# Graph product with layer norm: the product chunks of a pair of units gathered beside one lower row

## The chip, the cores and the metric

The kernel runs on one core of one Trainium2 chip. The metric is the device time of one execution in microseconds (us). The profile adds what each engine did: PE is TensorE's matrix work, PEld its weight loads, DVE is VectorE, ACT ScalarE, POOL GpSimd, SP SyncE, which issues most of the loads.

## The reference

For each of 8 batches there are x (2048x64) and adj (2048x2048). U (2048x16) gives one gate matrix for all batches.

```
Ws = 0.5 * (W + jnp.swapaxes(W, -1, -2))
A = jax.nn.sigmoid(U @ U.T)
K = Ws * A[None, :, :]
deg = jnp.maximum(K.sum(axis=-1), EPS)
d = jax.lax.rsqrt(deg)
K = K * d[:, :, None] * d[:, None, :]
return w_scale * jnp.einsum('bnm,bmc->bnc', K, x)
```

The result is added to x, and each row of 64 is normalised (mean, variance). All is in float32.

## The kernel before

**Tiles.** A batch's adj is cut into 4x4 units of 512x512, each held in a tile K[(i, j)] as four rows (r = 0 to 3) of 128x512. A unit has one home; the next batch's unit is loaded over it when its product is done.

**Lower rows.** The work of a batch goes over 40 lower rows (`LOWER`, 10 steps of 4 rows). For lower row g, TensorE transposes the mirrored blocks into a bank of the tile tw (L280: 4 transposes of 128x128, on a diagonal step 1, 2, 3 and 4, that is on rows 0 to 3, 8 to 11, 32 to 35 and 36 to 39). VectorE adds tw to K's row ("add g", L481), and then multiplies by the gate with a row sum ("gate g", L491). VectorE's order is add g, gate g-1, add g+1, gate g. tw has three banks, so that transposes of row g wait for add g-3 (`bank_free`, L270).

**Upper rows.** Row r of step s is, at row number 4(s+1)+r+2 (six after its lower row), transposed back into the tile kt (L294, 4 transposes; on diagonal steps 3, 2, 1, 0) and copied by ScalarE with a row sum (L410). The first of a step waits for all four gates of its step (L289): the upper row at row 14 for gate 11, at 18 for gate 15, at 26 for gate 23, at 34 for gate 31.

**Products.** The einsum is 16 unit products, in 8 pairs (`PAIRS`), each pair in four chunks c. One chunk is one call of `product`: two matmuls with 64 columns of output each, one on either half of the array (L309, 128x512 moving), two records each. Pairs 0 to 3 of batch b run beside its own lower rows (`OWN_ROWS`; `FIRST_OWN_ROWS` in batch 0), pairs 4 to 7 are carried into batch b+1 (`CARRIED_ROWS`). The three lists give for each of 16 chunks the number of the lower row. Rows 40 to 45 have no lower row: upper rows and products alone.

**Order.** TensorE's order at one row number is: tw transposes, product chunks listed for it, kt transposes. At row 5 stand eight transposes of y of batch b-2 before those of tw (L332), whose results VectorE scales (L528). GpSimd adds x, centres and divides (L222, L226, L233) beside VectorE's rows; mean and variance are taken by VectorE at rows 11 and 15. Degrees and z (L499, L511) stand at rows 24 and 25, 33 and 34, and at the end of a batch.

**Loads.** SP loads a pair's units of the next batch when `prod_done` says that the pair is finished (L192). VectorE, ScalarE, GpSimd and SP have written orders too. Batches 0 and 1 are written out apart (no y of an earlier batch in batch 1, no carried products in batch 0); batches 2 to 7 are the loop. Batch 7's carried pairs stand behind the loop (L390).

Of the kernel before, what the change touches and what calls it, by code (L numbers as in the profile page):

```python
# [14 lines left out]
G = 4  # L15
# [41 lines left out]


OWN = 4
OWN_ROWS = [28, 28, 30, 31, 32, 33, 34, 36, 38, 39, 39, 40, 45, 45, 45, 45]  # L60
FIRST_OWN_ROWS = [28, 29, 30, 31, 32, 33, 34, 35, 36, 38, 39, 40, 45, 45, 45, 45]
CARRIED_ROWS = [2, 4, 4, 5, 7, 8, 10, 11, 13, 15, 17, 18, 18, 21, 22, 24]
UPPER_LAG = 2


# [21 lines left out]
def bass_graph_resnorm_kernel(nc, x, adj, u, w_scale, out):  # L87
# [6 lines left out]
    with ExitStack() as ctx:  # L94
# [167 lines left out]
        def _(pe):  # L262
# [35 lines left out]
            def product(b, q, c, stage=2):  # L298

                if c == 0:  # L300
                    if q in Z_OF_PAIR:
                        pe.wait_ge(z_ready, NZ * b + (Z_OF_PAIR[q] + 1))
                    if q == 0 and stage == 0:
                        pe.wait_ge(gate_ready, NL)
                    elif q == 0:
                        pe.wait_ge(y_copied, 2 * b)
                for n, m in PAIRS[q]:
                    at = (m % 2) * C
                    t = pe.matmul(yp[at:at + C, m // 2, :], z[:, n * G + c, :], K[(n, m)][:, c, :],  # L309
                                  start=(q == first_unit[m] and c == 0), stop=(q == last_unit[m] and c == G - 1))  # L310
                if c == G - 1:
                    t.then_inc(prod_done, 1)
# [22 lines left out]
            def outer_product(g):  # L335

                s, r = LOWER[g]
                i, j = STEPS[s]
                if g >= 2:
                    pe.wait_ge(gate_ready, g - 1)  # L340
                w = lower_width(s, r)
                pe.matmul(yp[:, g % 2, 0:w], ut_a[:, (i * G + r) * P:(i * G + r + 1) * P],  # L342
                          ut_b[:, j * UW:j * UW + w], start=True, stop=True).then_inc(uu_done, 1)

            def steps(b, stage):
# [3 lines left out]
                for at in range(NL + G + 2):  # L349
# [4 lines left out]
                    if at < NL and stage == 0:  # L354
                        for g in range(gates_before(at), gates_before(at + 1)):
                            outer_product(g)
                    for part, row in zip(carried, CARRIED_ROWS):
                        if row == at and stage:
                            product(*part, stage=stage)
                    for part, row in zip(own, OWN_ROWS if stage else FIRST_OWN_ROWS):  # L360
                        if row == at:
# [292 lines left out]
```

## Time and profile before

| what | value |
| --- | --- |
| time, median of 3 runs | 559.32 us (559.29 to 559.76) |
| span of the profiled execution | 557.6 us |
| PE busy | 95% of the span, 3208 instructions |
| VectorE busy | 78%, 1113 instructions |
| ScalarE busy | 39% |
| GpSimd busy | 18% |
| DMA | 142.98 MB, mean 256 GB/s |

The span runs from the first to the last instruction of the profiled execution; the median time of the runs is 1.7 us longer, which is what lies around the span. A time of the trace is counted from the span's start. Busy times of TensorE contain overlaps of pipelined matmuls.

### The profile page before, as it was taken

What the parts mean: (1) busy time and instruction counts of PE and PEld (TensorE: products, weight loads), DVE (VectorE), ACT (ScalarE), POOL (GpSimd) and SP (SyncE); (2) the same over time, 40 slices, a digit from 0 to 9 for tenths busy, and PEclk for the clock granted to TensorE, in tenths of its full rate; (3) what the DMA queues carried; (4) which work ended last, traced back from release to release, by engine and by line L of the source; (5) the groups of instructions that cost most, each with busy time, mean ns of one, the idle gap of its engine ahead of it and who ended that gap; (6) DMA issues with size and microseconds to landing.
All of it is one profiled execution on the core that took longest, in us unless ns stands there. A gap on an engine that the chain in (4) does not pass through costs nothing.

```text
span 557.6 us, 9999 instructions
## 1 busy us (share of the span) xinstructions
PE 530.7 (95%) x3208; PEld 296.0 (53%) x3208; DVE 433.7 (78%) x1113; ACT 217.9 (39%) x654; POOL 99.3 (18%) x61
## 2 busy tenths in 40 slices
PE   4899999999999999999999999999999999999991
PEld 4685445654556545555456544665456554564430
DVE  5898566875999659985799759997599956997554
ACT  2894413532245414344145332444134531444311
POOL 0000010001150013300214011410133002130153
PEclk9999999999999999999999999999999999999997
DMA  8997899758977699578985879776996688945003
GB/s 272 387 332 274 292 341 300 248 207 297 338 250 244 215 352 316 211 201 291 356 280 209 269 275 352 226 260 201 356 319 240 188 299 320 321 171 168 1 0 75
DMA packets 102850, 142.98 MB, mean 256 GB/s; under 512 B 37296, under 2 KB 37296, under 8 KB 102832
## 3 DMA queue, kind: packets, MB, share of 16 engines
q1 hardware_dynamic: 88240, 139.08, 71.7%
q10 hardware_dynamic: 14592, 3.67, 3.6%
q8 instruction: 10, 0.16, 0.1%
q14 instruction: 8, 0.07, 0.0%
HBM read 138.54 MB, written 4.19 MB: 256 GB/s over the span
## 4 chain that ended last, share of the span: by engine, by line
PE 80%; DVE 8%; issue 6%; ACT 3%; POOL 1%; DMA 1%; POOLq 0%; DVEq 0%
PE yp L309 39%; PE kt L294 21%; PE tw L280 17%; DVE k L481 3%; DVE k L491 2%; ACT k L410 1%; ACT gate L401 1%; PE yp L342 1%; DMA h<-in_L_gnn_U_dram 1%; PE tw L332 1%; DVE h L528 1%; DVE z L511 1%; PE tw L374 0%; POOL h L222 0%; PE yp L374 0%
## 5 line engine op out<-in xcount | busy, mean ns | idle before, releaser
L410 ACT ACTIVATE k<-kt 128x512 f32<-128x512 f32 (+3 forms) x288 | 151.7, 528 | 297.5 <-PE kt L294 292.6
L309 PE MATMUL yp<-k,z 128*64 128x512 f32 x960 | 247.5, 612 | 2.8 <-DVE z L511 2.8
L481 DVE TENSOR_TENSOR k<-tw,k 128x512 f32<-128x512 f32 (+2 forms) x320 | 193.4, 606 | 33.8 <-PE tw L280 30.5
L491 DVE CUSTOM_DVE_ANT_0 k<-k,gate 128x512 f32<-128x512 f32 (+2 forms) x320 | 217.2, 681 | 0.3 <-ACT gate L401 0.3
L294 PEld LDWEIGHTS kt<-ident,k 128*128 128x128 f32 x960 | 106.2, 140 | 128.7 <-ACT k L410 90.3
L280 PE MATMUL tw<-ident,k 128*128 128x128 f32 x1088 | 169.5, 275 | 2.7 <-DVE k L481 1.2
L294 PE MATMUL kt<-ident,k 128*128 128x128 f32 x960 | 157.8, 282 | 1.7 <-ACT k L410 1.7
L280 PEld LDWEIGHTS tw<-ident,k 128*128 128x128 f32 x1088 | 126.1, 140 | 30.5 <-issue 13.2
L309 PEld LDWEIGHTS yp<-k,z 128*64 128x64 f32 x960 | 52.1, 135 | 64.2 <-issue 58.6
L239 POOL TENSOR_TENSOR d<-deg,minus_half 128x4 f32<-128x4 f32 (+1 forms) x24 | 29.2, 1217 | 316.8 <-DVE deg L501 316.8
L410 ACT ACTIVATION_READ_ACCUMULATOR k<-kt 128x1 f32 x288 | 57.1, 198 | 0.0
L499 DVE TENSOR_REDUCE deg<-deg_parts 128x4 f32<-128x20 f32 (+1 forms) x24 | 4.3, 181 | 47.8 <-ACT k L410 47.8
L231 POOL TENSOR_TENSOR rstd<-var,minus_half 128x16 f32<-128x16 f32 x7 | 20.4, 2911 | 36.3 <-DVE var L542 36.3
L491 DVE DVE_READ_ACCUMULATOR2_ANT deg_parts<- 128x1 f32 x320 | 25.9, 81 | 0.0
L511 DVE TENSOR_TENSOR z<-xt,d 128x256 f32<-128x256 f32 (+1 forms) x24 | 12.4, 515 | 16.7 <-POOL d L239 16.7
L222 POOL TENSOR_TENSOR h<-h,x_keep 128x1024 f32<-128x1024 f32 x7 | 16.5, 2357 | 47.3 <-DVE h L528 47.3
L226 POOL TENSOR_TENSOR h<-h,mean 128x1024 f32<-128x1024 f32 x7 | 13.3, 1901 | 47.4 <-DVE mean L535 47.4
L401 ACT ACTIVATE gate<-yp 128x512 f32<-128x512 f32 (+3 forms) x40 | 20.4, 552 | 1.7 <-PE yp L342 1.2
L342 PE MATMUL yp<-ut_b,ut_a 128*128 128x512 f32 (+3 forms) x40 | 16.1, 439 | 1.3 <-ACT gate L401 1.1
L233 POOL TENSOR_TENSOR h<-h,rstd 128x1024 f32<-128x1024 f32 x7 | 15.9, 2269 | 0.5
L390 PE MATMUL yp<-k,z 128*64 128x512 f32 x64 | 14.2, 595 | 0.0
L528 DVE TENSOR_TENSOR h<-tw,f 128x512 f32<-128x512 f32 x14 | 9.0, 686 | 3.7 <-PE tw L332 3.7
(60 smaller groups left out, 116.3 us busy)
## 6 DMA issues: line engine op xcount, KB each, us to landing
k<-in_adj_dram SPq DMA_DIRECT2D x128, 1024.0 KB, 7.2
xt<-in_x_dram ACTq DMA_DIRECT2D x7, 512.0 KB, 7.0
out_dram<-h SPq DMA_DIRECT2D x7, 512.0 KB, 8.7
xt<-in_x_dram SPq DMA_DIRECT2D x1, 512.0 KB, 14.1
out_dram<-k SPq DMA_DIRECT2D x2, 256.0 KB, 2.6
h<-in_L_gnn_U_dram SPq DMA_DIRECT2D x1, 128.0 KB, 4.3
ws<-in_L_gnn_w_scale_dram ACTq DMA_DIRECT2D x1, 0.5 KB, 2.9
```

Of the source, the lines that this page charges most:

```text
L222: nc.gpsimd.tensor_tensor(h[:, :, :], h[:, :, :], x_keep[:, :, :], ALU.add).then_inc(h_ready, 1)
L231: nc.gpsimd.tensor_tensor(rstd[:, :], var[:, :], minus_half[:, :], ALU.pow).then_inc(rstd_ready, 1)
L239: nc.gpsimd.tensor_tensor(d[:, s], deg[:, s], minus_half[:, s], ALU.pow).then_inc(d_ready, 1)
L280: t = pe.transpose(tw[:, tw_bank(g), c * P:(c + 1) * P], K[(j, i)][:, c, r * P:(r + 1) * P], ident[:, :])
L294: t = pe.transpose(kt[:, g % RING, k * P:(k + 1) * P], K[(i, j)][:, c, r * P:(r + 1) * P], ident[:, :])
L309: t = pe.matmul(yp[at:at + C, m // 2, :], z[:, n * G + c, :], K[(n, m)][:, c, :], start=(q == first_unit[m] and c == 0), stop=(q == last_u ...
L342: pe.matmul(yp[:, g % 2, 0:w], ut_a[:, (i * G + r) * P:(i * G + r + 1) * P], ut_b[:, j * UW:j * UW + w], start=True, stop=True).then_inc(u ...
L401: nc.scalar.activation(A[:, A_AT[g]:A_AT[g] + w], yp[:, g % 2, 0:w], ACT.Sigmoid).then_inc(gate_ready, 1)
L410: nc.scalar.activation(K[(j, i)][:, r, c0:UW], kt[:, g % RING, 0:UW - c0], ACT.Copy, accum_out=deg_parts[:, n, part:part + 1]).then_inc(up ...
L481: nc.vector.tensor_tensor(row, tw[:, tw_bank(g), 0:w], row, ALU.add).then_inc(sum_done, 1)
L491: nc.vector.tensor_tensor_reduce(row, row, A[:, A_AT[g]:A_AT[g] + w], 1.0, 0.0, ALU.mult, ALU.add, deg_parts[:, i * G + r, j:j + 1]).then_ ...
L511: nc.vector.tensor_tensor(z[:, n0:n1, :], xt[:, n0:n1, :], per_row(d, n0, n1), ALU.mult).then_inc(z_ready, 1)
```

## The change

The three lists are replaced. The pairs keep their order, and the chunks their count: 16 own and 16 carried per batch. The four chunks of a pair now share one row number: own pairs at rows 29, 35, 40 and 45, carried pairs at 3, 9, 15 and 21. Nothing else in the kernel is touched.

```diff
 OWN = 4
-OWN_ROWS = [28, 28, 30, 31, 32, 33, 34, 36, 38, 39, 39, 40, 45, 45, 45, 45]
-FIRST_OWN_ROWS = [28, 29, 30, 31, 32, 33, 34, 35, 36, 38, 39, 40, 45, 45, 45, 45]
-CARRIED_ROWS = [2, 4, 4, 5, 7, 8, 10, 11, 13, 15, 17, 18, 18, 21, 22, 24]
+OWN_ROWS = [row for row in (29, 35, 40, 45) for _ in range(G)]
+FIRST_OWN_ROWS = [row for row in (29, 35, 40, 45) for _ in range(G)]
+CARRIED_ROWS = [row for row in (3, 9, 15, 21) for _ in range(G)]
```

Only TensorE's order differs. At the start of the loop's body (rows 0 to 5 of a batch) its instructions stand so, with - before and + in the change; x2 of L309 is one chunk, x8 a whole pair, and L280's first five transposes are rows 0 to 2 but the first, L302 the wait for z, L326 that for y:

```order
 L280 MATMUL tw<-ident,k 128x128 x5
+L270 REGISTER_ALU
+L280 MATMUL tw<-ident,k 128x128 x4
 L302 ISA
-L309 MATMUL yp<-k,z 64x512 x2
-L270 REGISTER_ALU
-L280 MATMUL tw<-ident,k 128x128 x4
-L270 REGISTER_ALU
-L280 MATMUL tw<-ident,k 128x128 x4
-L309 MATMUL yp<-k,z 64x512 x4
+L309 MATMUL yp<-k,z 64x512 x8
+L270 REGISTER_ALU
+L280 MATMUL tw<-ident,k 128x128 x4
 L326 ISA
```

The chunk at row 2 has moved behind row 3's transposes, and those that stood at rows 4 and 5 have moved ahead of row 4's.

Later in the same body, from row 28 on, TensorE had chunks at nearly every row:

```order
 L280 MATMUL tw<-ident,k 128x128 x4
 L302 ISA
-L309 MATMUL yp<-k,z 64x512 x4
-L291 REGISTER_ALU
-L294 MATMUL kt<-ident,k 128x128 x4
-L270 REGISTER_ALU
-L280 MATMUL tw<-ident,k 128x128 x4
-L291 REGISTER_ALU
-L294 MATMUL kt<-ident,k 128x128 x4
-L270 REGISTER_ALU
-L280 MATMUL tw<-ident,k 128x128 x4
-L309 MATMUL yp<-k,z 64x512 x2
```

In the change rows 29 to 35 stand so (row 29's four tw transposes are just ahead of this, those of row 35 the last L280):

```order
+L309 MATMUL yp<-k,z 64x512 x8
+L291 REGISTER_ALU
+L294 MATMUL kt<-ident,k 128x128 x4
+L270 REGISTER_ALU
+L280 MATMUL tw<-ident,k 128x128 x4
+L291 REGISTER_ALU
+L294 MATMUL kt<-ident,k 128x128 x4
+L270 REGISTER_ALU
+L280 MATMUL tw<-ident,k 128x128 x4
+L291 REGISTER_ALU
+L294 MATMUL kt<-ident,k 128x128 x4
+L270 REGISTER_ALU
```

The pair's eight matmuls are together between row 29's transposes and row 29's upper row, and no product stands between there and row 35.

## Rows read from the trace of the kernel before

**Rows 1.** The page: the span, and busy time by engine.

```profile
span 557.6 us, 9999 instructions
PE 530.7 (95%) x3208; PEld 296.0 (53%) x3208; DVE 433.7 (78%) x1113; ACT 217.9 (39%) x654; POOL 99.3 (18%) x61
```

**Rows 2.** Busy time by stretch, batch 4: PE, PEld, DVE, ACT, POOL, clock, DMA.

```profile
267.80:274.40 6.60, 6.60 (x42) 3.66 (x42) 5.38 (x16) 0.00 (x0) 0.00 (x0) 1.00 1.02 359
274.40:314.20 39.80, 39.03 (x249) 22.82 (x246) 38.94 (x90) 17.21 (x50) 10.50 (x5) 1.00 0.76 256
314.20:333.25 19.05, 19.05 (x107) 8.83 (x106) 9.29 (x34) 7.38 (x26) 2.64 (x2) 1.00 0.77 276
```

**Rows 3.** Groups by line, 274.4 to 314.2 us: busy, mean ns, idle before.

```profile
L481 DVE TENSOR_TENSOR k<-tw,k 128x512 f32<-128x512 f32 (+3 forms) x27 | 17.6, 653 | 0.0
L499 DVE TENSOR_REDUCE deg<-deg_parts 128x4 f32<-128x20 f32 x1 | 0.2, 174 | 0.8 <-ACT k L410 0.8
```

**Rows 4.** Timeline, TensorE's weight loads around a chunk, then around a pair.

```profile
253.85 0.42 PEld L294 LDWEIGHTS kt<-ident,k 128*128 128x128 f32 x4 [0.81 <-ACT k L410]
255.42 0.20 PEld L309 LDWEIGHTS yp<-k,z 128*64 128x64 f32 x4 [0.17 <-issue]
256.43 0.42 PEld L294 LDWEIGHTS kt<-ident,k 128*128 128x128 f32 x4 [0.81 <-ACT k L410]
...
264.21 0.20 PEld L309 LDWEIGHTS yp<-k,z 128*64 128x64 f32 x4
267.80 0.64 PEld L280 LDWEIGHTS tw<-ident,k 128*128 128x128 f32 x6 [0.81 <-issue]
```

**Rows 5.** Timeline, VectorE's pace over full rows: add 21, gate 20, add 22.

```profile
299.15 0.68 DVE L481 TENSOR_TENSOR k<-tw,k 128x512 f32<-128x512 f32 x1
299.76 0.67 DVE L491 CUSTOM_DVE_ANT_0 k<-k,gate 128x512 f32<-128x512 f32 x1
300.37 0.68 DVE L481 TENSOR_TENSOR k<-tw,k 128x512 f32<-128x512 f32 x1
```

**Rows 6.** Timeline around row 28: add 25, tw 28, two chunks, tw 29, add 29.

```profile
305.28 0.69 DVE L481 TENSOR_TENSOR k<-tw,k 128x512 f32<-128x512 f32 x1
306.03 0.42 PEld L280 LDWEIGHTS tw<-ident,k 128*128 128x128 f32 x4 [0.30 <-DVE k L481]
307.05 0.20 PEld L309 LDWEIGHTS yp<-k,z 128*64 128x64 f32 x4 [0.61 <-DVE z L511]
309.31 0.47 PEld L280 LDWEIGHTS tw<-ident,k 128*128 128x128 f32 x4
310.54 0.69 DVE L481 TENSOR_TENSOR k<-tw,k 128x512 f32<-128x512 f32 x1
```

**Rows 7.** Timeline, row 39: from its transposes to the add that waited.

```profile
324.74 0.47 PEld L280 LDWEIGHTS tw<-ident,k 128*128 128x128 f32 x4
325.48 0.69 DVE L481 TENSOR_TENSOR k<-tw,k 128x512 f32<-128x512 f32 x1 [1.02 <-PE tw L280]
```

**Rows 8.** Timeline, y's scaling, add 5, and GpSimd beside gate 4.

```profile
273.20 1.29 DVE L528 TENSOR_TENSOR h<-tw,f 128x512 f32<-128x512 f32 x2 [0.52 <-PE tw L332]
274.40 0.68 DVE L481 TENSOR_TENSOR k<-tw,k 128x512 f32<-128x512 f32 x1
274.65 2.35 POOL L222 TENSOR_TENSOR h<-h,x_keep 128x1024 f32<-128x1024 f32 x1 [7.43 <-DVE h L528]
275.00 2.55 DVE L491 CUSTOM_DVE_ANT_0 k<-k,gate 128x512 f32<-128x512 f32 x1
```

**Rows 9.** Timeline, gate 11, the upper row that waits for it, and gate 18.

```profile
285.09 2.00 DVE L491 CUSTOM_DVE_ANT_0 k<-k,gate 128x512 f32<-128x512 f32 x1
287.22 0.31 PEld L294 LDWEIGHTS kt<-ident,k 128*128 128x128 f32 x3 [0.51 <-issue]
296.23 1.78 DVE L491 CUSTOM_DVE_ANT_0 k<-k,gate 128x512 f32<-128x512 f32 x1
```

**Rows 10.** Timeline: add 30 of batches 0 and 4, first transposes of batches 1 and 2.

```profile
51.02 0.69 DVE L481 TENSOR_TENSOR k<-tw,k 128x512 f32<-128x512 f32 x1
311.75 0.69 DVE L481 TENSOR_TENSOR k<-tw,k 128x512 f32<-128x512 f32 x1
73.11 0.64 PEld L280 LDWEIGHTS tw<-ident,k 128*128 128x128 f32 x6 [0.81 <-issue]
136.88 0.88 PE L280 MATMUL tw<-ident,k 128*128 128x128 f32 x6
```

## The prediction

> **What bounds the kernel now.** I first read the page [rows 1]: TensorE is busy in 95% of the span, VectorE in 78%. That alone would say that whatever shortens TensorE shortens the kernel. So I next cut one batch of the loop into three stretches [rows 2]: rows 0 to add 5, add 5 to the end of row 31, rows 32 to 44 with their products. In the first and the third TensorE works without a pause and VectorE has room (9.3 us busy in 19.05). In the middle one, 39.8 us long, VectorE is busy for 38.9, and its groups by line [rows 3] show no idle time before the 27 additions, and 0.8 us before the degrees. There VectorE sets the pace, and TensorE runs as far ahead as tw's three banks let it: at row 28 its transposes start when add 25 is over [rows 6]. A batch is 65.45 us: batch 4 starts at 267.80 [rows 4] and batch 2 at 136.88 [rows 10], 130.92 / 2.
>
> **Prices.** Between transposes, 13 transposes and the way into a chunk take 255.42 - 253.85 = 1.57 us, and the chunk with the way out 1.01 [rows 4]. A pair in one block, with the way out, takes 267.80 - 264.21 = 3.59. Three chunks more cost 2.58, so one is 0.86 and the way out 0.15. A transpose is 0.11 (a weight load of four takes 0.42 to 0.47 in [rows 4, 6], the six of row 0 to 2 0.64 [rows 4]), so 13 are 1.44 and the way in is 0.13. One product block costs 0.285 us beyond its chunks. VectorE takes 0.605 for an addition or a gate of 512 columns, 1.21 a row [rows 5]; rows of 384, 256 and 128 columns I take in proportion at 0.95, 0.68 and 0.42. An addition frees its bank 0.75 after its start (305.28 to 306.03 [rows 6]), and can start 0.74 after the first of its four transposes (324.74 to 325.48 [rows 7]).
>
> **What the change removes.** Blocks: from 13 in batch 0 and 25 in each of the seven others, 188, to 4 + 7 x 8 = 60. 128 x 0.285 = 36.5 us of TensorE's time. No chunk, transpose, load or addition is added or taken away. VectorE's, ScalarE's, GpSimd's and SP's orders stay.
>
> **What it adds.** A block is now 3.44 us of products at once. While it runs, VectorE lives on the rows transposed ahead. Take full rows, TensorE as far ahead as the banks allow, and S the start of tw of row r, freed by add r-3. The block starts at S + 0.44 + 0.13, kt of row r at S + 4.16, tw of row r+1 at S + 4.56, and add r+1 can start at S + 5.30. VectorE, which began add r-3 at S - 0.75, has eight operations before it, and would want to start it at S - 0.75 + 8 x 0.605 = S + 4.09. So it stands idle for 1.2 us at every such block. Before, row 28 had two chunks: there tw 29 starts at 309.31 and add 29 could start at 310.05, but starts at 310.54 [rows 6], because VectorE was not ready: 0.49 to spare. Two chunks more, 1.72, turn that into 1.23 of idle, the same number. This idle time falls in the stretch in which VectorE is the bound, and nothing gives it back there. Queued behind the waiting addition are all later rows, and TensorE waits for them by its banks.
>
> **One loop batch, worked through,** in us from its first transpose, before in brackets. The ledger takes each start as the later of its engine's turn and its wait.
> - Entry: rows 0 to 3 and a whole block stand ahead of tw 4 (before, one chunk, then two). tw 4 starts at 4.9, add 4 at 5.6, y's scaling at 6.8, add 5 at 8.0 (6.6, [rows 8]): +1.4. GpSimd still holds gate 4 for 1.9 us beyond its usual 0.67 [rows 8], so add 6 starts at 11.1.
> - Block 9: tw 9 waits for add 6 until 11.85, though TensorE has been free since 9.1. The block runs to 15.8, and tw 10 gives add 10 at 16.4, where VectorE is ready at 14.9 (rows 8 and 9 are narrow): +1.5.
> - Block 15: kt 14 waits for gate 11, held up by GpSimd as before [rows 9]. add 16 starts at 27.9, VectorE would be ready at 27.2 (the variance stands ahead): +0.7.
> - Block 21: GpSimd's last operation holds a gate (1.1 us now, gate 18 [rows 9]); whether that or the block is late, tw 22 is done for 36.8. add 22 (32.6 before: 300.37 in [rows 5]): together +4.2, so +0.6 here.
> - Block 29: add 30 waits 1.2, of which 0.7 comes back, since VectorE no longer waits for ScalarE before the degrees and for z: +0.5. add 30 is at 48.7 (311.75 - 267.80 = 43.95, [rows 10]): +4.75.
> - From add 30 on TensorE is the bound. tw 30 starts at 48.0; then come 72 - 4 = 68 transposes, 7.5, twelve chunks, 10.3, three blocks' 0.85, tw 30's own 0.4, and 0.8 in which kt 34 waits for gate 31, because rows 30 to 34 have no product in between. The next batch starts at 68.0, 19.3 after add 30 (21.5 before): -2.2.
>
> Sum: 4.75 - 2.2 = +2.5 us a batch, for batches 2 to 7: +15.2. The saved blocks are not lost: ten of the 17 lie in rows 0 to 29, where TensorE only waits longer.
>
> **Batches 0 and 1.** Batch 0 has only block 29 in VectorE's stretch. add 30 is at 51.02 and batch 1 starts at 73.11, 22.1 later [rows 10]; now 1.2 later and then 19.3: -1.6. Batch 1 has no y, mean and variance, so VectorE is ahead of its rows more often and TensorE is the bound in most of it. By the same ledger its blocks 3, 9, 15, 21 and 29 end at 4.9, 12.7, 21.2, 29.8 and 41.7, tw 30 starts then after kt 29 at 42.1, and 20.0 more (68.0 - 48.0) make 62.1, instead of 136.88 - 73.11 = 63.8: -1.6. What follows the loop is the same. Total: 15.2 - 3.2 = +12.0. On the span of 557.6 that gives 569.6; the runs shown have a median 1.7 above that span, so **571.3 us**.
>
> The loads cost nothing: every pair ends in the same row as before or up to three rows earlier. The tightest, the unit (3,0) freed with carried pair 5, now has block 9 to row 16, about 12 us, where rows 11 to 16 did before.
>
> **Rivals.**
> - *TensorE is the bound after all, and the whole saving comes home.* For it: 95% busy. Against: [rows 2, 3]. It gives 559.3 - 36.5 = 522.8. The Trainium skill, TensorEngine Tiling (Array Packing), under key properties, says that a change of tiling mode drains TensorE; our products use half arrays and the transposes the whole one. The price of 0.285 in the rows fits such a drain, and by this rule alone 128 fewer drains would be that gain. Chance 0.03.
> - *VectorE's queue lasts through the blocks* (the banks or TensorE's order let it have more rows than I think). Then the 1.5, 0.7, 0.6 and 1.2 us of idle are not there: 4 us off each loop batch, which turns +2.5 into -1.5, and 1.2 off batch 0: 559.3 - 9 - 2.8 - 1.6 = about 546. The sign turns when the four blocks together cost VectorE less than 1.5 us a batch. Against it stands the check at row 28. Chance 0.10.
> - *The losses are half of mine*, by waits that overlap with the GpSimd collisions (1.9, 1.3 and 1.1 us a batch in [rows 8, 9]): no net difference, 559. Chance 0.05.
> - *TensorE's clock falls.* It is granted at 1.00 in all three stretches [rows 2], the 2.4 GHz level. The ledger has TensorE waiting 2.7 us ahead of tw 9 and some 2.2 ahead of kt 14, where waits of before are under 1 us [rows 6, 9]. If block 9 ran at 1.2 GHz, its 3.44 us would double on the path: 6 x 3.4 = 20.6 more, 592. Chance 0.07. The Trainium skill, TensorE: Matmul & The Clock Gate, on PE-mode transpose, says that transposes don't count as activity for the clock in the way that matmuls do, which would make the new stretches without products worse still; no row here has so long a stretch of transposes alone in the loop.
>
> **How the numbers follow.** The forecast has the remaining 0.75. Its own bounds: each block's idle time between 0.8 and 1.5 gives +/- 1.5 us a batch, 9 in all, if all err alike: 562 to 580. The range reaches a little lower toward the rivals, 560 to 579, and leaves out 546 and less and the fallen clock, 0.2 together. Slower by over 0.2% (about what a measurement of this kernel tells from no change): 0.82; within: 0.05; faster: 0.13.
>
> **What the changed profile would show.** 60 blocks of products; a period of 68.0 us; in the middle stretch idle time of 3 to 4.5 us a batch before L481 released by L280, at additions 10, 16 or 22, and 30, where it was 0.0; TensorE's waits for VectorE's additions of about 2.5 us ahead of row 9; TensorE's busy share down to some 87%, VectorE's busy time unchanged at 434 us; add 5 at 8.0 after the batch's start. I am wrong if additions find their rows transposed through the blocks, if the batch is shorter than 65.4, or if the clock in the middle stretch is under 1.

## The result, and the profile after

The changed kernel takes 588.4 us in the median of 4 runs (582.1 to 591.8), against 559.3 (558.8 to 559.8). The ratio is 1.048, with a 95% interval of 1.042 to 1.054. The ratio leaves out the longest of the four runs; the other three have a median of 586.0. The forecast was 571.3, with a range of 560 to 579: the direction was right, the size was not. The runs scatter by 10 us where those of before scatter by 1, and the granted clock goes with the time: 0.974 at 582.1 us, 0.968 at 586.0, 0.963 at 590.8, 0.960 at 591.8.

The head of the page after, to be read beside [rows 1] (the third line is the granted clock in 40 slices of the span):

```profile
span 580.0 us, 9999 instructions
PE 509.7 (88%) x3208; PEld 310.6 (54%) x3208; DVE 432.3 (75%) x1113; ACT 215.6 (37%) x654; POOL 97.8 (17%) x61
PEclk9999999999999999999999998899989999899996
```

TensorE is busy for 21 us less, and yet the span is 22 us longer. The clock dips from slice 25 on. Batch 4 lies before the first dip. Its three stretches, that of rows 0 to add 5, that from there on and the rest (compare [rows 2]):

```profile
268.95:276.95 8.00, 7.44 (x48) 4.29 (x47) 5.30 (x16) 0.00 (x0) 0.00 (x0) 1.00 1.05 389
276.95:316.10 39.15, 33.06 (x224) 21.30 (x222) 36.74 (x83) 15.95 (x46) 10.08 (x5) 1.00 0.74 242
316.10:336.78 20.68, 20.03 (x126) 11.43 (x124) 11.55 (x40) 8.40 (x30) 2.65 (x2) 1.00 0.71 251
```

The clock is 1.00 throughout, and the batch is 336.78 - 268.95 = 67.83 us long; the ledger said 68.0. VectorE's additions of this batch in time order: add 5, and behind it those that waited for their transposes:

```profile
276.95 0.68 DVE L481 TENSOR_TENSOR k<-tw,k 128x512 f32<-128x512 f32 x1
...
285.30 0.56 DVE L481 TENSOR_TENSOR k<-tw,k 128x384 f32<-128x384 f32 x1 [1.42 <-PE tw L280]
...
296.75 0.69 DVE L481 TENSOR_TENSOR k<-tw,k 128x512 f32<-128x512 f32 x1 [0.57 <-PE tw L280]
...
305.66 0.69 DVE L481 TENSOR_TENSOR k<-tw,k 128x512 f32<-128x512 f32 x1 [0.32 <-PE tw L280]
...
317.42 0.69 DVE L481 TENSOR_TENSOR k<-tw,k 128x512 f32<-128x512 f32 x1 [1.12 <-PE tw L280]
```

The lines are additions 5, 10, 16, 22 and 30. From the batch's start they stand at 8.0, 16.35, 27.8, 36.7 and 48.5 us, against the ledger's 8.0, 16.4, 27.9, 36.8 and 48.7. Where before VectorE never waited for tw in this stretch [rows 3], it now waits once behind every block, 3.4 us in all. TensorE waits in other places, its weight loads show where:

```profile
280.76 0.20 PEld L280 LDWEIGHTS tw<-ident,k 128*128 128x128 f32 x2 [2.65 <-DVE k L481]
291.34 0.31 PEld L294 LDWEIGHTS kt<-ident,k 128*128 128x128 f32 x3 [2.82 <-issue]
```

The first is tw of row 9, which waits for add 6. The second is the upper row of row 14, which waits for gate 11 (the releaser is not named on this row). Before, the same two rows had to wait less than 1 us ([rows 9] for the second).

Now batch 5. GpSimd's first operation stands at the same place of every batch (8.25 us after the start in batch 4), so its starts measure the batches. They follow here from batch 4 to batch 7, and behind them stand four windows of batch 5: block 9, the time before the second pause, the pause, block 15. The granted clock is the third number from the end:

```profile
277.20 2.35 POOL L222 TENSOR_TENSOR h<-h,x_keep 128x1024 f32<-128x1024 f32 x1 [8.82 <-DVE h L528]
345.02 2.35 POOL L222 TENSOR_TENSOR h<-h,x_keep 128x1024 f32<-128x1024 f32 x1 [8.82 <-DVE h L528]
416.80 2.35 POOL L222 TENSOR_TENSOR h<-h,x_keep 128x1024 f32<-128x1024 f32 x1 [8.82 <-DVE h L528]
488.53 2.35 POOL L222 TENSOR_TENSOR h<-h,x_keep 128x1024 f32<-128x1024 f32 x1 [8.82 <-DVE h L528]
```

```profile
347.80:351.80 4.00, 3.21 (x8) 1.06 (x10) 3.90 (x14) 1.46 (x5) 0.00 (x0) 0.59 1.13 341
356.00:358.50 2.50, 2.18 (x20) 1.94 (x18) 2.47 (x6) 2.07 (x6) 0.31 (x1) 1.00 0.90 344
358.50:360.70 2.20, 0.00 (x0) 0.00 (x0) 2.20 (x4) 0.58 (x1) 1.59 (x1) 1.00 1.05 399
360.70:366.00 5.30, 5.23 (x19) 2.04 (x21) 4.88 (x11) 1.06 (x3) 0.31 (x1) 0.68 0.17 61
```

From batch 4 to batch 5 it is 67.8 us (as from 2 to 3 and from 3 to 4), from 5 to 6 71.8, from 6 to 7 71.7. In batch 5 the clock falls to its level of 1.2 GHz twice, each time just behind one of the two pauses, in block 9 (0.59 in the mean of the window) and in block 15 (0.68). In batch 4 the same two pauses left it at 1.00. So a batch costs 67.8 us at full clock and 71.8 with both falls. In this execution the clock fell in three batches, 5, 6 and 7, twice in each (the last is 3.9 us longer too, against the filled kernel below): 580.0 - 11.7 = 568.3, where the ledger had 569.6.

### The profile page after: what moved, and what is told of

Same layout as the page of the kernel before. It is cut to its first block, busy times and chain, and to the rows that moved or that the text cites. A ratio compares the mean times of both kernels' runs of the same rounds, so it can differ in the third digit from the quotient of the medians.

```text
span 580.0 us, 9999 instructions
## 1 busy us (share of the span) xinstructions
PE 509.7 (88%) x3208; PEld 310.6 (54%) x3208; DVE 432.3 (75%) x1113; ACT 215.6 (37%) x654; POOL 97.8 (17%) x61
## 4 chain that ended last, share of the span: by engine, by line
PE 60%; DVE 18%; issue 14%; ACT 4%; POOL 1%; DMA 1%; POOLq 0%; DVEq 0%
PE yp L309 39%; PE tw L280 11%; PE kt L294 9%; DVE k L481 8%; DVE k L491 5%; ACT gate L401 2%; ACT k L410 1%; DVE mean L533 1%; DVE h L528 1%; DVE deg_parts L491 1%; DMA h<-in_L_gnn_U_dram 1%; PE yp L342 1%; POOL h L222 0%; PE tw L374 0%; PE yp L374 0%
## 5 line engine op out<-in xcount | busy, mean ns | idle before, releaser
L309 PE MATMUL yp<-k,z 128*64 128x512 f32 x960 | 228.2, 619 | 0.0
L280 PE MATMUL tw<-ident,k 128*128 128x128 f32 x1088 | 170.2, 277 | 23.6 <-DVE k L481 19.6
L294 PE MATMUL kt<-ident,k 128*128 128x128 f32 x960 | 151.5, 277 | 26.8 <-DVE deg_parts L491 24.4
L280 PEld LDWEIGHTS tw<-ident,k 128*128 128x128 f32 x1088 | 125.5, 141 | 49.4 <-DVE k L481 24.4
L294 PEld LDWEIGHTS kt<-ident,k 128*128 128x128 f32 x960 | 110.3, 140 | 66.7 <-issue 52.1
L309 PEld LDWEIGHTS yp<-k,z 128*64 128x64 f32 x960 | 65.6, 141 | 119.9 <-issue 119.0
L422 ACT ACTIVATE y_sb<-h 128x1024 f32<-128x1024 f32 x7 | 7.4, 1058 | 20.6 <-POOL h L226 20.6
L233 POOL TENSOR_TENSOR h<-h,rstd 128x1024 f32<-128x1024 f32 x7 | 14.4, 2056 | 0.5
L390 PE MATMUL yp<-k,z 128*64 128x512 f32 x64 | 14.2, 595 | 0.0
```

Source lines behind the costliest of these rows:

```text
L233: nc.gpsimd.tensor_tensor(h[:, :, :], h[:, :, :], per_row(rstd, 0, NC), ALU.mult).then_inc(normed, 1)
L280: t = pe.transpose(tw[:, tw_bank(g), c * P:(c + 1) * P], K[(j, i)][:, c, r * P:(r + 1) * P], ident[:, :])
L294: t = pe.transpose(kt[:, g % RING, k * P:(k + 1) * P], K[(i, j)][:, c, r * P:(r + 1) * P], ident[:, :])
```

## Experiments

**Filling the pauses.** In the changed kernel, extra transposes of the upper row already in hand fill TensorE's pauses (they write into the bank of kt what it gets anyway, so the output is unchanged):

```diff
 UPPER_LAG = 2
+FILL = {(0, 2): 22, (1, 3): 22}
...
+                if stage == 2:
+                    for k in range(FILL.get((s, r), 0)):
+                        c = chunks[k % len(chunks)]
+                        pe.transpose(kt[:, g % RING, (k % len(chunks)) * P:(k % len(chunks) + 1) * P],
+                                     K[(i, j)][:, c, r * P:(r + 1) * P], ident[:, :])
```

> The change, with 22 extra transposes in each loop batch behind the upper row of row 8 and 22 behind that of row 13, which write once more what their bank of kt gets anyway: they fill TensorE's pauses ahead of row 9's transposes (2.65 us) and ahead of gate 11's upper row (2.8 us) and put nothing on the path. Theory 1, the pauses let the clock fall: the clock stays at 1.00 through the loop, every loop batch takes 67.8 us as batches 2 to 4 did, 569 to 571 us in all, and the runs agree within 0.3%. Rival, the long stretches without products let it fall, and transposes do not hold it up: falls as in the change, 582 to 592 us.

Measured: 571.5 us (569.9 to 573.4), ratio to before 1.022 (1.019 to 1.026). GpSimd's first operation recurs every 67.85 us in all batches of the loop. The windows are block 9, block 15 and the whole of the eight batches' rows:

```profile
348.00:352.00 4.00, 3.98 (x19) 1.26 (x18) 3.18 (x12) 0.73 (x4) 0.00 (x0) 1.00 1.17 299
359.50:364.00 4.50, 4.50 (x26) 1.91 (x25) 3.96 (x10) 1.04 (x5) 0.43 (x1) 1.00 0.00 0
20.00:540.00 520.00, 500.39 (x3326) 321.29 (x3325) 407.17 (x1061) 201.19 (x633) 83.72 (x48) 1.00 0.76 261
```

The clock never falls, though the stretches without products are as long as in the change. 264 added transposes make the kernel 17 us faster than the change. The rival is out: it is the pauses. The scatter of 3.5 us is wider than the 0.3% expected, and its source is open.

**Filling one pause.** The same with `FILL = {(0, 2): 22}`.

> The change with only row 8's 22 extra transposes: the pause ahead of row 9's transposes is filled, that ahead of gate 11's upper row (2.8 us) stays. Theory: the remaining pause can still let the clock fall, once a batch at most, just behind it (block 15) and never in block 9; 3.9 us for two falls in the change makes some 2 us for each, so 571 to 583 us, with runs that scatter. Rival, it takes both pauses within a batch: no fall, 571 us as with both filled.

Measured: 581.9 us (578.6 to 582.3). The two windows are block 9 and block 15 of batch 2:

```profile
145.00:149.00 4.00, 4.00 (x19) 1.31 (x20) 3.07 (x11) 0.73 (x4) 0.00 (x0) 1.00 1.12 294
155.50:160.00 4.50, 4.47 (x17) 1.85 (x19) 4.50 (x10) 1.02 (x3) 0.00 (x0) 0.67 0.26 96
```

Where the pause is filled the clock stays, where it is left the clock falls. The intervals between batches are 70.2, 69.9, 70.2, 67.9 and 70.0 us, so one fall at block 15 costs 2.0 to 2.4 us, 2.2 in the mean, which leaves 1.7 of the change's 3.9 for that at block 9. Each pause acts by itself; the kernel with the carried half alone, below, shows single falls of both kinds.

**Halving both pauses.** `FILL = {(0, 2): 11, (1, 3): 11}`.

> The change with 11 extra transposes at row 8 and 11 at row 13: both pauses are cut from 2.65 and 2.8 us to about 1.4 and 1.6. Theory, it is the length of the pauses that decides: no fall, 571 us. Rival, any pause of that kind at these places will do (before has none above 1 us): falls, 575 to 592 us.

Measured: 570.8 us (570.5 to 571.3). The pause ahead of row 9 is now

```profile
281.63 0.20 PEld L281 LDWEIGHTS tw<-ident,k 128*128 128x128 f32 x2 [1.47 <-DVE k L487]
```

the second pause is 1.6 us by the same view, and the batches are all 67.8 us. Pauses of 1.5 and 1.6 us at these places cost no clock.

**The change itself once more,** for its scatter.

> The changed kernel itself once more. Theory: a run's time above 570 us goes with the number of batches in which the clock falls, 3.9 us each, none to six: runs between 570 and 594 us, the granted clock lower where the time is longer. Rival, the time above 570 us has another source: no such order of clock and time.

Measured: 590.1 us. Its runs, with their clocks: 583.5 (0.971), 589.9 (0.963), 590.3 (0.963), 591.1 (0.963). In the profiled one (589.9) the first interval is 67.8 us, the next four 71.7: the clock falls in batches 3 to 7, where in the first profiled execution (582.1) it fell in batches 5 to 7. In both, every batch behind the first fallen one fell too, so what differs is how early the first fall comes. No run breaks the order of clock and time in either set of four.

**One half of the change.** First only `OWN_ROWS` and `FIRST_OWN_ROWS` as in the change, then only `CARRIED_ROWS`:

```diff
-CARRIED_ROWS = [row for row in (3, 9, 15, 21) for _ in range(G)]
+CARRIED_ROWS = [2, 4, 4, 5, 7, 8, 10, 11, 13, 15, 17, 18, 18, 21, 22, 24]
```

> Only the own pairs are gathered (29, 35, 40, 45), the carried chunks stand as before. Theory (ledger): add 30 is late by 1.2 - 0.7 = 0.5 us, then 2.2 us are saved where TensorE is the bound: -1.7 us in each of six loop batches, -1.6 in batch 0, -1.2 in batch 1: 546 us, with the clock never down in the loop, because no long pause of TensorE arises at rows 28 to 45. Rival, gathering costs wherever it is done: 559 or more.

Measured: 551.2 us (550.2 to 552.1), ratio 0.984 (0.982 to 0.988), which is 5 us above the 546 expected. A batch takes 64.5 us. The wait behind block 29 is there, in batch 3:

```profile
236.39 0.17 DVE L499 TENSOR_REDUCE deg<-deg_parts 128x4 f32<-128x20 f32 x1 [0.76 <-ACT k L410]
...
244.37 0.69 DVE L481 TENSOR_TENSOR k<-tw,k 128x512 f32<-128x512 f32 x1 [1.12 <-PE tw L280]
```

It costs its full 1.1 us: the 0.76 before the degrees, which comes back in the change (idle 0.0 there), does not come back here. That is most of the difference between -0.9 a batch and the -1.7 expected. The gathered own pairs are worth 8 us as they are.

> Only the carried pairs are gathered (3, 9, 15, 21), the own chunks stand as before. Theory (ledger): add 22 is 4.1 us late, 0.5 comes back before the degrees, nothing after it: +3.6 us in six loop batches, -1 in batch 1: 580 us at full clock, plus 3.9 us for each batch in which the clock falls at its two pauses, so 580 to 603. Rival, VectorE's queue bridges the blocks and only the 70 saved blocks count: 559.3 - 20 = 539.

Measured: 590.9 us (590.1 to 594.3), ratio 1.058. Batches without a fall are 69.2 us long, 3.8 above before (3.6 expected); each of the others has one fall. The windows are block 9 of batch 3 and block 15 of batch 6:

```profile
217.00:223.00 6.00, 5.59 (x18) 1.67 (x18) 3.52 (x12) 1.07 (x5) 0.00 (x0) 0.72 0.85 225
439.00:445.00 6.00, 5.91 (x23) 2.19 (x23) 4.90 (x11) 1.08 (x3) 0.99 (x1) 0.72 0.15 56
```

The fall at block 9 makes its batch 1.7 us longer, that at block 15 2.4. The whole loss of the change and more is in the carried half.

**One block in VectorE's stretch.** The lists of before, with the last four carried chunks at 21.

> The lists of before, with the last four carried chunks (18, 21, 22, 24) all at row 21: one whole block in the stretch where VectorE is the bound. Theory: VectorE stands idle some 1.2 us before add 22 with L280 as releaser, of which up to 0.7 comes back at the waits before the degrees and for z; +0.5 to +0.9 us in six batches, -0.9 in batch 1: 561 to 564 us, clock full. Rival, TensorE is the bound there: three blocks less in seven batches, 559.3 - 6.0 = 553.

Measured: 560.5 us (559.2 to 561.9, 10 runs), ratio 1.0015 (0.9999 to 1.003). A batch is 65.65 us, +0.2. VectorE waits 0.46 before add 22 instead of the 1.2 of the rule. One of the operations ahead of that addition, gate 18, is held beside GpSimd's last operation:

```profile
296.37 1.78 DVE L491 CUSTOM_DVE_ANT_0 k<-k,gate 128x512 f32<-128x512 f32 x1
```

It takes 1.1 us more than the usual 0.67, so VectorE wants add 22 that much later; TensorE began row 21's transposes 0.4 us later than the rule has it: 1.2 + 0.4 - 1.1 = 0.5. The wait before the degrees is gone. The time is below the 561 to 564 us expected, and its interval holds no change at all; the length of a batch has the direction expected, with a third of the size. The rival (553) is out.

**Blocks where they are free.** Own rows 28, 28, 30, 30, then pairs at 35, 40, 45; the carried list of before.

> The lists of before with blocks only where TensorE is the bound: own rows 28, 28, 30, 30, then whole pairs at 35, 40 and 45, in batch 0 too; the carried chunks as before. Theory: two chunks at a row leave VectorE its 0.49 us to spare, so no idle time before additions 29 and 31; behind add 30 six blocks fewer in seven batches, 6 x 0.285 = 1.7 us each, eight in batch 0, 2.3: 559.5 - 14.3 = 545 us. Rival, the saving is eaten by the wait of the upper row for gate 31 or by ScalarE's copies, which limit the transposes between the blocks: 552 or more.

Measured: 548.3 us (548.0 to 548.5), ratio 0.980 (0.978 to 0.981), where 545 was expected. A batch is 64.2 us. Two groups of two within three rows do cost VectorE something, 0.77 us before addition 31. The next kernel changes the carried list too, two chunks at each of the rows 5, 7, 9, 11, 14, 16, 19 and 22:

> As the kernel with blocks in the tail only, and the carried chunks two by two at rows 5, 7, 9, 11, 14, 16, 19 and 22. Theory: two at a row cost VectorE nothing, and with no product ahead of row 4's transposes add 5 starts about 5.1 us after the batch's first transpose instead of 6.6, which is up to 1.5 us a batch where VectorE is the bound; some of it is lost where TensorE, with all 16 carried chunks now behind add 5, falls behind: 1 us in six batches, 539 us (range 536 to 545). Rival, the stretch behind add 5 turns TensorE-bound, or unit (2,0), freed by row 7 now, lands too late for row 12: 545 or more.

Measured: 547.5 us (546.4 to 548.0), 63.7 a batch. That is above the range of 536 to 545 and in that of the rival. In batch 4 add 5 does come 1.2 us earlier than in the kernel before it (5.4 us after the batch's first transpose, against 6.6). But VectorE now waits 0.32, 0.39 and 0.42 us for the transposes of rows 10, 12 and 23, which it did not, and only 0.5 comes back before the degrees, so 0.5 a batch is left. The last pair moves the own rows to 28, 28, 32, 32, 36, 40, 45, with the carried list of before and with twos:

> As the kernel with blocks in the tail only, but own pair 0 at rows 28, 28, 32, 32 and pair 1 at 36. Theory: with no chunk at row 30, VectorE's 0.77 us of idle time before addition 31 goes, and the wait of row 34's upper row is partly covered by the chunks at row 32: 0.5 to 0.8 us less a batch, 543 to 545 us instead of 548.3. Rival, behind add 30 TensorE is the bound and a wait of VectorE there is worth nothing: 548.

> The same own rows, with the carried chunks two by two at 5, 7, 9, 11, 14, 16, 19, 22. Theory: the two gains add up: 0.5 us a batch below the kernel before it in this list, as the other pair of kernels stood to each other (63.7 to 64.2 us a batch): 541 to 544 us. Rival, they overlap: the same as the better one.

Measured: 545.3 us (544.7 to 545.4), ratio 0.973 (0.970 to 0.976), and 544.2 (542.7 to 544.6), ratio 0.970 (0.968 to 0.973). Both are a few tenths of a us above what was expected. Batches are 63.7 and 63.2 us. In the first the wait before addition 31 is gone; the two gains add up. In the second, TensorE does the same 3208 pieces of work with 23 us less busy time than before ([rows 1]), and 15 of them come off the span this time:

```profile
span 542.6 us, 9999 instructions
PE 507.6 (94%) x3208; PEld 306.2 (56%) x3208; DVE 430.9 (79%) x1113; ACT 217.9 (40%) x654; POOL 99.4 (18%) x61
```

This execution has one fall of the clock too, in batch 1, behind a pause shorter than those of the change. The lines are the end of that pause and a window 2 us later:

```profile
75.10 0.42 PEld L280 LDWEIGHTS tw<-ident,k 128*128 128x128 f32 x4 [2.17 <-DVE k L481]
77.00:78.00 1.00, 1.00 (x5) 0.03 (x2) 0.10 (x2) 0.00 (x0) 0.00 (x0) 0.50 1.06 393
```

The kernel with twos and the earlier pair has a pause of the same length there, and its clock stayed at 1.00.

## Why the prediction was wrong

- **The bound and the stretches** (right). VectorE sets the pace from add 5 to add 31; what TensorE saved (36.5 us by the prediction; its busy time, which holds the slower clock's longer matmuls too, fell by 21) became waiting of TensorE.
- **The price of a block, 0.285 us** (right in size). The kernel with blocks in its tail has six fewer a batch and gains 1.3 of 1.7 us, with 0.77 us of a new wait in it; with the later pair, which has six fewer too and not that wait, it is 1.7.
- **The ledger** (right). 67.8 us measured, 68.0 forecast for a batch at full clock; 62.3 measured and 62.1 forecast for batch 1. (The terms listed behind add 30 add up to 67.85, not to 68.0.) The kernel with its pauses filled, which is the change at full clock, takes 571.5, the forecast 571.3; so close a hit has some luck in it, since these runs scatter by 3.5. One term was not general: the 0.7 us that came back before the degrees does so here but not with the own half alone.
- **The clock** (the step that failed: the forecast put the cost of a falling clock at nothing). I worked out both pauses, 2.7 and 2.2 us (2.65 and 2.8 measured), and put the fall of the clock among the rivals with a chance of 0.07. For it to stay I had only that it is 1.00 in rows whose waits are under 1 us, which says nothing about pauses three times as long. The rival priced one fall, in block 9, at 3.4 us in all six batches and came to 592. Measured are two falls in an affected batch, 1.7 and 2.2 us, together 3.9, in three of the six loop batches of one profiled execution and in five of the other. They are cheaper than doubled blocks, because the clock is back before a block is over: in batch 5 block 9 runs from 349.2 to 354.1 us, and from 352 on the clock is 1.00 again. That the slowest runs come near the rival's 592 is luck, as its one fall was priced too high and the second left out. The prediction had named a clock under 1 in the middle stretch as a sign of being wrong, and it was.
- **The Trainium skill's rule** (TensorE: Matmul & The Clock Gate, on PE-mode transpose), that transposes do not count for the clock as matmuls do: as to holding the clock, the trace doesn't bear it out. Added transposes alone in the pauses held it at 1.00 in the whole loop. Whether transposes alone would raise a fallen clock, no run here shows.

Open: why the clock falls in batch 5 and not in batch 4 behind pauses of the same length. Run to run and batch to batch it differs; nothing in the kernel does. Nor is it shown how short a pause must be to be safe: 1.6 us never cost the clock in the profiled execution with half-filled pauses, 2.2 us did once and once did not.

## What to carry to other kernels

Gather small pieces of work that cost an engine a switch only where that engine is the bound: there six blocks fewer were worth 1.3 to 1.7 us a batch, while the same gathering, in the stretch where the other engine lives on three banks, cost 3.8. And where an estimate shows TensorE a new pause of about 2 us or more ahead of matmuls that lie on the path, take the slower clock as a likely case, and not as a remote one; if the order can't be changed, work thrown away in the pause is cheaper than the pause.

## What was not expected of the hardware

TensorE's clock fell behind pauses of 2.65 and 2.8 us, but not in every batch, once behind one of 2.2, and in no profiled batch behind pauses of 1.5 us; a fall on the path of the loop cost 1.7 to 2.4 us. The run's time therefore scattered over 10 us, while kernels without such pauses in the loop scattered by 0.5 to 3.5. Once the clock had fallen in a batch of the change, it fell in every later one.
